# Feed-forward stage of an attention and mixed-expert kernel: weight slots, residual buffers, the last batch's normalisation and the last run's output

## What is computed

```python
x = x + _layernorm(_L0_attn_ref(_layernorm(x), w_qkv))        # windowed attention, 16 heads
x = x + _layernorm(_L0_ffn_ref(_layernorm(x), ...))           # the stage that is changed

# _L0_ffn_ref, x viewed as 4 batches here, F = 2048, 8 experts
g   = (relu(x @ gate_w1.T + gate_b1) @ gate_w2.T + gate_b2).mean(axis=1)   # [batch, 8]
mW1 = W1 + einsum('be,efh->bfh', g, TW1);  mb1 = b1 + g @ Tb1
mW2 = W2 + einsum('be,ehf->bhf', g, TW2);  mb2 = b2 + g @ Tb2
u   = gelu(x @ mW1.T + mb1)
out = u @ mW2.T + mb2
```

## Time and profile before

| | us |
|---|---|
| median of 3 runs | 3087.42 |
| lowest and highest | 3071.88, 3089.4 |
| the profiled execution | 3080.82 |
| its span, from the first to the last instruction | 3078.9 |
| PE busy in the span | 2904.6 (94%) |
| last matmul starts | 3046.84 |
| last store issued | 3073.03 |

### The profile page before, as it was taken

How to read it: one execution, slowest core, us unless ns; L and a number is a source line. 1 busy time by engine, 2 the same in 40 slices (tenths; PEclk the granted TensorE clock), 3 DMA queues, 4 the chain that set the end, 5 groups by cost and what they waited for, 6 DMA issues and landing times.

```text
span 3078.9 us, 55797 instructions
## 1 busy us (share of the span) xinstructions
PE 2904.6 (94%) x20444; PEld 2418.1 (79%) x20444; DVE 1984.1 (64%) x3732; ACT 1737.0 (56%) x3398; POOL 870.8 (28%) x773
## 2 busy tenths in 40 slices
PE   7999999699999999959889999999999999999995
PEld 6888888588888888847777888788887888878884
DVE  4333333278887888857757787776768766796632
ACT  2222222166666667645545666766667666776665
POOL 0000000188887888853310000320006000140004
PEclk9999999799999999979999999999999999999998
DMA  5545554668887887669999777876669655895612
GB/s 194 182 170 177 196 186 164 174 161 193 192 196 182 194 193 193 165 211 361 352 356 332 261 273 252 333 282 235 220 225 388 242 205 206 307 348 204 215 40 96
DMA packets 385299, 697.07 MB, mean 226 GB/s; under 512 B 27912, under 2 KB 160008, under 8 KB 385048
## 3 DMA queue, kind: packets, MB, share of 16 engines
q1 hardware_dynamic: 362912, 635.14, 65.1%
q0 software_dynamic: 9472, 33.56, 2.9%
q10 hardware_dynamic: 12672, 25.17, 2.2%
HBM read 525.45 MB, written 167.78 MB: 225 GB/s over the span
## 4 chain that ended last, share of the span: by engine, by line
PE 42%; DMA 4%; DVE 3%; POOL 2%; ACT 2%; SPq 2%; issue 1%; ACTq 0%; POOLq 0%; DVEq 0%
PE e_hid L1194 7%; PE e_hid L1195 7%; PE e_hid L1196 7%; PE e_acc L1211 7%; PE e_acc L1212 7%; PE e_acc L1213 7%; DMA yl_scratch<-e_yt_lo 3%; POOL e_sums L1114 1%; DVE e_part L1497 1%; DVE e_yt_lo L1447 1%; SPq L976 1%; DVE e_c_stats L1420 1%; DMA e_x<-x_scratch 1%; ACT e_sums L1351 0%; DVE e_c_y L1441 0%
## 5 line engine op out<-in xcount | busy, mean ns | idle before, releaser
L1497 DVE SCALAR_TENSOR_TENSOR e_part<-e_ring,e_g_cols,e_part 128x512 f32<-128x512 f32 x896 | 637.2, 768 | 2.1
L666 DVE TENSOR_REDUCE b_neg_max<-b_ps_score 128x1 f32<-128x384 f32 (+1 forms) x1024 | 491.6, 527 | 73.0 <-PE b_ps_score L531 61.7
L637 ACT ACTIVATE b_probs<-b_ps_keys 128x384 f32<-128x384 f32 (+1 forms) x1024 | 426.9, 478 | 84.4 <-PE b_ps_keys L546 56.9
L1309 ACT ACTIVATE e_u<-e_hid,e_mb 128x512 f32<-128x512 f32 x256 | 177.2, 692 | 436.5 <-PE e_hid L1196 431.1
L1521 DVE TENSOR_TENSOR e_u_lo<-e_u,e_u_hi 128x512 fp32r<-128x512 f32 x256 | 193.0, 754 | 324.2 <-ACT e_u_hi L1313 324.1
L1102 POOL TENSOR_SCALAR e_var<-e_moments 128x4 f32<-128x4 f32 x16 | 8.8, 549 | 1213.2 <-DVE e_moments L1533 1212.3
L531 PE MATMUL b_ps_score<-b_k_st,b_q_st 96*128 96x384 f32 (+1 forms) x1024 | 333.6, 366 | 16.0 <-DMA b_q_st<-qk_scratch 15.7
L491 POOL TENSOR_TENSOR b_total<-b_probs 128x512 f32<-128x512 f32 x256 | 323.9, 1282 | 70.0 <-ACT b_probs L637 70.0
L546 PE MATMUL b_ps_keys<-b_q_st,b_k_st 97*128 97x384 f32 (+1 forms) x1024 | 314.3, 349 | 28.0 <-DMA b_q_st<-b_max_rows 26.7
L237 DVE TENSOR_TENSOR a_qk<-a_acc,a_qk 128x512 fp32r<-128x512 f32 x128 | 88.5, 692 | 345.4 <-ACT a_qk L176 345.4
L501 POOL TENSOR_TENSOR b_total<-b_total,b_probs 128x512 f32<-128x512 f32 x224 | 286.3, 1278 | 64.8 <-ACT b_probs L637 62.3
(11 more groups left out here) (137 smaller groups left out, 6325.3 us busy)
## 6 DMA issues: line engine op xcount, KB each, us to landing
e_ring<-mix_rows SPq DMA_DIRECT2D x558, 512.0 KB, 5.2
qk_scratch<-a_qk SPq DMA_DIRECT2D x128, 512.0 KB, 2.8
b_k_st<-qk_scratch SPq DMA_DIRECT2D x192, 256.0 KB, 4.4
b_q_st<-qk_scratch SPq DMA_DIRECT2D x192, 256.0 KB, 4.2
a_x_in<-x SPq DMA_DIRECT2D x16, 1024.0 KB, 7.2
v_scratch<-a_v SPq DMA_DIRECT2D x64, 256.0 KB, 3.0
b_v_sb<-v_scratch SPq DMA_DIRECT2D x64, 256.0 KB, 4.9
o_scratch<-b_out SPq DMA_DIRECT2D x128, 128.0 KB, 2.9
```

Source lines behind the costliest of these rows:

```text
L637: act.activation(probs[:, m % RING, h, 0:(hi - lo) * WIN], ps_keys[x % BANKS][:, 0:(hi - lo) * WIN], ACT.Exp, scale=SCALE).then_inc(exp_do ...
L666: dve.tensor_reduce(neg_max[:, g % 2, i, h:h + 1], ps_score[y % BANKS][:, 0:(hi - lo) * WIN], AX_X, ALU.max, negate=True).then_inc(reduced, 1)
L1497: dve.scalar_tensor_tensor(out=part[:, n % 2, half, :], in0=ring[:, slot, :], scalar=g_cols[:, b, e:e + 1], in1=so_far, op0=ALU.mult, op1= ...
```

## The change

- `W_RING` goes from 5 to 4: four slots of mixed weights.
- `x1` becomes two buffers of a whole chunk. SP loads them in one transfer of 1 MB each (`load_x1`), the first two before the feed-forward's first steps, the one for closing at + 2 at the place in SP's program that belongs to six steps after the last step of closing `at`, once its adds are done (`next_x1`). POOL issues no load.
- POOL computes the root and shift of the next closing of the same batch between the second and the third add of the current one.
- DVE takes the row statistics of a closing before the low half of that step, not after it.
- The closings of the last batch (12 to 14; `LATE` is 12) are normalised by DVE (`late_normalise`) two steps after the run's last, not by ACT. POOL computes only the root for them.
- The last run (closing 15) is not copied to `sums`. DVE takes its statistics from the `acc` banks, ACT the square root, DVE the reciprocal and the shift. Tiles 0 and 1 are then normalised by ACT and added to x1 by POOL, tiles 2 and 3 by DVE for both. Each tile is stored by its own transfer, from ACT's queue and SP's.

```diff
-W_RING = 5
+W_RING = 4
@@ phase_gate_ffn
+    LAST = RUNS - 1
+    LATE = PER * (BATCH - 1)
+    HALF_TILES = TILES // 2
-        x1 = sb("x1", [P, TILES, D], F32)
+        x1 = sb("x1", [P, 2, TILES, D], F32)
+        def load_x1(eng, at):
+            i = at % 2
+            eng.dma_start(x1[:, i], x1_dram[tokens(closing[at]), :].rearrange("(t p) d -> p t d", p=P)).then_inc(x1_loaded[i], 16)
@@ sync
+                def next_x1(at):
+                    sp.wait_ge(added, TILES * (at + 1))
+                    load_x1(sp, at + 2)
                 store_mb2(1)
+                load_x1(sp, 0)
+                load_x1(sp, 1)
                 refill_half(3)
                 for s in range(STEPS):
                     refill(upto[s - 1] if s else EXPERTS * START, upto[s])
...
+                        if s == last[run] + 6 and closes(run) and closed_before(run) + 2 < len(closing):
+                            next_x1(closed_before(run))
...
+                for t in range(HALF_TILES, TILES):
+                    sp.wait_ge(end_high_added, t - HALF_TILES + 1)
+                    sp.dma_start(end_rows(t, t + 1), sums[:, runs[LAST][1], t:t + 1, :]).then_inc(end_stored, 16)
@@ gpsimd
-                for at, r in enumerate(closing):
...
-                    for t in range(TILES + 1):
...
-                        if t and at + 1 < len(closing):
-                            pool.wait_ge(added, TILES * at + t)
-                            load_x1(closing[at + 1], t - 1)
+                for at, r in enumerate(closing[:-1]):
+                    if at % PER == 0:
+                        root(at)
+                    for t in range(TILES):
+                        add_rows(at, t)
+                        if t == 1 and at < LATE and (at + 1) % PER:
+                            root(at + 1)
                     pool.wait_ge(added, TILES * (at + 1))
                     pool.dma_start(out[tokens(r), :]...)
+                    if at >= LATE and at + 2 < len(closing):
+                        root(at + 1)
+                end = len(closing) - 1
+                pool.wait_ge(x1_loaded[end % 2], 16 * (end // 2 + 1))
+                for t in range(HALF_TILES):
+                    pool.wait_ge(end_scaled, t + 1)
+                    rows = sums[:, runs[LAST][1], t, :]
+                    pool.tensor_tensor(rows, rows, x1[:, end % 2, t, :], ALU.add).then_inc(end_low_added, 1)
@@ scalar
-                        if s == last[r]:
+                        if s == last[r] and r != LAST:
                             next_run(r)
-                        if s == last[r] + 3 and closes(r):
+                        if s == last[r] + 3 and closes(r) and closed_before(r) < LATE:
                             normalise(r)
+                act.activation(unused[:, 0:1], eps[:, :], ACT.Sqrt).then_inc(table_ready, 1)
+                act.wait_ge(end_ready, 1)
+                act.activation(var[:, end % 2, :], moments[:, end % 2, :, 1], ACT.Sqrt, bias=eps[:, :]).then_inc(end_std_done, 1)
+                act.wait_ge(end_shift_done, 1)
+                for t in range(HALF_TILES):
+                    act.activation(sums[:, runs[LAST][1], t, :], acc[t][:, :], ACT.Identity, bias=shift[...], scale=rstd[...]).then_inc(end_scaled, 1)
+                for t in range(HALF_TILES):
+                    act.wait_ge(end_low_added, t + 1)
+                    act.dma_start(end_rows(t, t + 1), sums[:, runs[LAST][1], t:t + 1, :]).then_inc(end_stored, 16)
@@ vector
+                def late_normalise(r):
+                    dve.wait_ge(rstd_done, at + 1)
+                    for t in range(TILES):
+                        dve.tensor_scalar(rows, rows, moments[:, i, t, 0:1], rstd[:, i, t:t + 1],
+                                          ALU.subtract, ALU.mult).then_inc(late_norm_done, 1)
+                def end_stats():
+                    for t in range(TILES):
+                        dve.wait_ge(used, TILES * (STEPS - 1) + t + 1)
+                        dve.bn_stats(stats[:, i, t, :], acc[t][:, :]).then_inc(stats_chain, 1)
...
+                def end_tiles():
+                    dve.wait_ge(end_std_done, 1)
+                    dve.reciprocal(rstd[:, i, :], var[:, i, :]).then_inc(end_rstd_done, 1)
...
+                    for t in range(HALF_TILES, TILES):
+                        dve.tensor_scalar(rows, acc[t][:, :], moments[:, i, t, 0:1], rstd[:, i, t:t + 1], ...)
+                        dve.wait_ge(end_norm_done, t - HALF_TILES + 1)
+                        dve.tensor_tensor(rows, rows, x1[:, i, t, :], ALU.add).then_inc(end_high_added, 1)
@@ the DVE loop over steps
-                    if 2 <= s and s + AHEAD < STEPS:
-                        low_hidden(s + AHEAD)
                     for r in range(RUNS):
                         if s == last[r] + 1 and closes(r):
                             row_stats(r)
+                        if s == last[r] + 2 and closes(r) and closed_before(r) >= LATE:
+                            late_normalise(r)
+                    if 2 <= s and s + AHEAD < STEPS:
+                        low_hidden(s + AHEAD)
...
-                row_stats(RUNS - 1)
+                end_stats()
+                end_tiles()
```

89 lines of the change are left out of this document (61 added, 28 removed).

## The result

The changed kernel takes 3057.87 us (median of 6 runs, 3055.41 to 3063.27), the kernel before 3082.72 us beside it (6 runs). The ratio is 0.9924, 95% interval 0.9903 to 0.9945: 0.8% faster, within the 1% that I called no change. The profiled execution took 3063.27 us, its span 3061.4.

What follows compares the result with a forecast made beforehand. PE, busy 94% of the span, was taken as the bound. Start 0.5, boundaries -3 and end -17.5 sum to -20.0 us: 3060.8 from the profiled 3080.82; the median may reach 3067.4, so 3064, own range 3056 to 3074.

Steps and rivals of the forecast that it cites:

- The end: After the last matmul: tail of 14.2 us instead of 31.7, so -17.5 us, bounds -20 and -10.
- The drawn chain: Last chunk's stations: normalise done 3049.5, aggregates 3052.3, factors 3053.1, adds 3057.2, store 3060.2, span's end 3061.4.
- The extra +2 us for POOL beside VectorE: Late normalise of closing 14: POOL's adds beside it delay VectorE by 2 us, between +0 and +3.8.
- The boundaries: Three changes of batch, 23.1 us lost before: -3 us, all at the first; bounds -23 and +36.
- The second and third boundary: Later batch changes: nothing won, as VectorE runs later; second's normalise at 2365.7 against 2364.80 before.
- The start: First feed-forward steps: 2 MB of x1 ahead of the weight loads costs +0.5 us, bounds 0 and 2.6.
- Four slots: Weight slots cut from five: no effect, since blocks still finish ahead with 43 us of cover, 33 for odd blocks.
- The boundaries did not heal (0.23): Rival at the batch changes: x1 lands in 6.5 us, VectorE's lag ends, 15 to 23 us return; chance 0.23.
- The rival of an end that stays long: After the last matmul: full exclusion, stores no faster than 5 us, tail only -10, total -7.4; chance 0.16.
- The rival of a slow x1: Third closing's x1 takes 24.2 us at each boundary: +39 us on the sum, 3103 or so; chance 0.06.
- the rule quoted in the prediction: DMA queues: POOL's transfers have their own turn, so x1 on SyncE's queue lands on the range's long side.

Runs made afterwards that it cites:

- tail_only: The kernel before with only the end part of the change put in: its end took 21.7 us, the gain is 0.2%.
- root_first: The changed kernel with POOL's root of a batch's fourth closing ahead of the third's adds: 0.9862 of the kernel before.
- ring4: The kernel before with four weight slots instead of five and nothing else: ratio interval 0.9996 to 1.0032.
- adds_wait14: The changed kernel with POOL's adds of closing 14 waiting for all four normalised tiles: last add 8.7 us behind the last matmul, 9.1 in the changed kernel.

## Why the prediction was right, step by step

The forecast was 3064 with 3056 to 3074 as its own range, by -20.0 us from the profiled execution. It came to 3057.87, -24.9 between the medians: inside the range, 1.9 us from its lower edge. Of the 6.1 us under the forecast, 1.3 are the level that I counted from (3064 is 20.0 under 3084; the median of six executions before is 3082.72), and 4.9 are terms that were too small. The terms, from the changed kernel's profile:

- **The end: -19.7 us, predicted -17.5.** The drawn chain is the one in the rows; each station came 0.8 to 1.1 us earlier than drawn, from its first one on: the statistics of closing 14 were ready 3.9 us ahead of the last matmul's end, not 3.0 as in the earlier trace rows, since VectorE now takes them ahead of the low half. Counted from the last matmul's end: late normalise begun at -2.4 (drawn -1.6) and done at 1.4 (2.3), aggregates 4.1 (5.1), factors 4.8 (5.9), last add 9.1 (10.0). The extra +2 us for POOL beside VectorE was right (3.83 us instead of 1.92). The rest of the miss is the close: the last 256 KB store landed 2.3 us after its issue and the span ended 0.5 us later, where I had 3.0 and 1.2.
- **But the step was priced to the wrong part.** I wrote the whole term to the end part, and the experiments split it into 9.9 for the end part alone and 7.5 for everything else alone. The working let POOL's root of closing 14 follow the statistics at once and had x1 of the last chunk there in time. It said that closings 12 and 13 end under PE's work "as before"; before, closing 13 was stored at 3052.98, 5.7 us behind the last matmul, and POOL had three closings left then, not two. What clears POOL and brings x1 in time (no loads on POOL, the second buffer, the earlier statistics) are conditions that the prediction never named; by its working, tail_only should have had an end of 14.2 and not 21.7. That the term came out at the right size is partly luck: the change happened to hold these conditions too.
- **The boundaries: -3.2 us in the two profiles, predicted -3.** Right in size and in place: one wait for the shift a boundary, at the fourth closing, behind x1 of the third. To compare the times, take off what the whole kernel ran later: at the first boundary its steps were 5.5 us later than before (step 56 at 1937.8 and 1932.3), 4.0 of that from ahead of the feed-forward and 1.5 from the start. Then x1 was issued at 1990.6, where I had 1990.5, landed 9.1 us later, not 11, and the fourth closing's normalise (2011.08) stood at 2005.6 where I had 2006.7; two adds took 3.0 and not 2.5. At the second boundary the steps were 1.8 us later: issue at 2348.0 (2349.5 foretold), normalise (2365.43) at 2363.6 (2365.7). Over the executions, before's order lost 25.2 us on average (three), the changed order 20.3 (five with the same boundary code: 19.6 to 21.2): -4.9, and 4.1 of that in the first boundary, where I had put it.
- **The second and third boundary.** I had the second down as VectorE's, because ScalarE waited there for mixing. root_first contradicts: against the changed kernel 8.4 us became 1.4 with nothing changed on VectorE's program. The trace of the kernel before had shown two things that I did not look at:

```profile
2354.42 4.75 DVE L1497 SCALAR_TENSOR_TENSOR e_part<-e_ring,e_g_cols,e_part 128x512 f32<-128x512 f32 x2
```

```profile
2362.58 0.61 POOL L1108 TENSOR_SCALAR e_shift<-e_shift 128x4 f32<-128x4 f32 x1
```

  The mixing was late because two of its operations took 4.75 us, not 1.40, while POOL made two adds and issued its loads. And POOL's shift was done at 2363.2, only 1.6 us before ScalarE's normalise (2364.80): without the wait for mixing, the wait for the shift would have come in its place. The last wait in a trace was not the one that a repair has to remove.
- **Not separated.** The change also takes the statistics ahead of the low half and moves POOL's loads away. No run takes one of these back alone, so their share in the first boundary's gain is not shown.
- **The start: +1.5 us in this execution, predicted +0.5** (bounds 0 and 2.6); an execution without it shows the other value, 0.
- **Four slots: nothing**, as ring4 shows.

With the averages in place of single executions the terms are -19.7 (end), -4.9 (boundaries) and +0.8 (start): -23.8, against -24.9 between the medians.

**The rivals.** The boundaries did not heal (0.23), but half of that rival was right: they can be healed, and one change of order does it. It named x1's landing and VectorE's lag as what decides; the landing did not have to get shorter, the root only had to stand ahead of it. The rival of an end that stays long (0.16) wanted stores of 5 us or more; they landed in 2.3 to 3.2 us, and the end fell by 19.7. The rival of a slow x1 (24.2 us) is contradicted: the third closing's load took 8.9 to 9.5 us in the changed kernel, and 8.5 to 14.8 in all the kernels that load it in one piece.

On the queues the rule quoted in the prediction (the Trainium skill, page "DMA: Bandwidth & Descriptors", section "SWDGE vs HWDGE vs iDMA"), as I read it there, would have given POOL's transfer the shorter landing. The measured 14.6 and 14.8 us on POOL's queue against 14.2 and 12.5 on SyncE's show no advantage here; POOL's had a 1 MB store right ahead of it.

## What to carry to other kernels

- Before you shorten a late transfer, look at what stands behind its wait on the same engine: four tiny instructions moved ahead of the wait were worth 16.5 us here, the earlier transfer 7.8 (14.4 from POOL's queue), and both together 7.4. Each is one execution's; those of the unchanged order differ by 1.6 us among themselves.
- A transfer or an engine that is late also keeps its followers out of others' way. Ask of each repair what will now run at the same time as what.
- When a change has several parts, price each part with the others absent too: the end's 19.7 us were 9.9 for the one part alone and 7.5 for the rest alone.

## What the runs showed of the hardware

POOL's 128x512 adds and VectorE's two-input operations hold each other up. It shows in several ways. Six mixing operations take 4.06 us alone and 1.03 us more for each add beside them (an undisturbed add takes 1.24), and the adds stretch too (3.44 us for two, against 2.50 in an undisturbed pair): they take turns. But a single VectorE operation that is ready once a row of adds is under way can wait for all of it: 4.89 us at 2369.63 beside four adds that ran in their undisturbed 4.95, and 2.90 us in adds_wait14. VectorE's one-input normalise in SBUF (0.54 us) is held as well (1.5 us); its statistics are not: from PSUM 2.48 and 2.49 us beside adds, from SBUF 2.46 us with POOL waiting (1995.64 in the changed kernel).

The Trainium skill, page "SBUF — State Buffer", section "SBUF: two separate sides", has the lock of the shared ports held for a whole instruction. The turns agree with it. The 4.89 us are more than one held instruction. As I read them, POOL got the ports four times in a row while VectorE waited; why it waits for the whole row there and takes turns in the mixing, no run shows.
